# Softmax totals of a gated cross-attention block: a VectorE sum of block-transposed p and one 16-column fp32 matmul, in place of two 512-column matmuls with a matrix of ones

## What is computed

```python
q = rope((layernorm(x) @ Wq).reshape(b, t, 32, 128))
k = rope((ctx @ Wk).reshape(b, t, 8, 128));  v = (ctx @ Wv).reshape(b, t, 8, 128)
logits = 30 * tanh(einsum('btkgd,bTkd->bkgtT', q, k) * 0.0884 / 30)
weights = softmax(where(mask, logits, -1e30), axis=-1)
x = x + tanh(g_xattn) * (einsum('bkgtT,bTkd->btkgd', weights, v).reshape(b, t, 4096) @ Wo)
# then x = x + tanh(g_ffn) * ffn(layernorm(x)), a gated silu block, inner size 1376, int4 weights
```

## Time and profile before

| what | value |
|---|---|
| median of 3 runs (lowest, highest) | 819.16 us (818.01 to 819.62) |
| the profiled execution: time, span | 819.05 us, 817.3 us |
| mean granted TensorE clock | 0.991 |
| PE busy | 785.6 us (96%) |
| DVE busy | 586.6 us (72%) |
| POOL busy | 492.8 us (60%) |
| ACT busy | 355.4 us (43%) |

### The profile page before, as it was taken

How to read it: one execution, slowest core, us unless ns; L and a number is a source line. 1 busy time by engine, 2 the same in 40 slices (tenths; PEclk the granted TensorE clock), 3 DMA queues, 4 the chain that set the end, 5 groups by cost and what they waited for, 6 DMA issues and landing times.

```text
span 817.3 us, 12587 instructions
## 1 busy us (share of the span) xinstructions
PE 785.6 (96%) x3937; PEld 654.8 (80%) x3937; DVE 586.6 (72%) x1224; ACT 355.4 (43%) x722; POOL 492.8 (60%) x392
## 2 busy tenths in 40 slices
PE   4889999999999999999999999999998689999998
PEld 3777888888888888888888888888887468888786
DVE  7797777777777777777777777776787677787531
ACT  3665444444334444444443443434444345555420
POOL 3689765566555666655665566656887466566400
PEclk9999999999999999999999999999999899999999
DMA  8320302010210201020102101120020034442011
GB/s 286 108 78 17 115 1 78 1 52 1 78 54 1 78 1 52 1 78 0 55 1 78 52 0 43 35 47 1 1 62 0 25 88 103 101 111 49 1 65 39
DMA packets 56989, 41.61 MB, mean 51 GB/s; under 512 B 22922, under 2 KB 44298, under 8 KB 56938
## 3 DMA queue, kind: packets, MB, share of 16 engines
q1 hardware_dynamic: 56938, 40.90, 17.3%
HBM read 38.77 MB, written 2.11 MB: 50 GB/s over the span
## 4 chain that ended last, share of the span: by engine, by line
PE 91%; DVE 5%; POOL 2%; issue 1%; ACT 1%; DMA 0%; DVEq 0%; POOLq 0%
PE ps_o L53 8%; PE ps_o L55 8%; PE ps_o L54 7%; PE bank_q L55 7%; PE bank_q L53 7%; PE bank_q L54 7%; PE ps_qT L1141 3%; PE bank_kv L53 3%; PE bank_kv L54 3%; PE bank_kv L55 3%; PE ps_s L54 3%; PE ps_s L53 3%; PE ps_s L55 3%; PE ps_pv L53 2%; PE ps_pv L54 2%; PE ps_pv L55 2%
## 5 line engine op out<-in xcount | busy, mean ns | idle before, releaser
L522 POOL TENSOR_TENSOR aT_lo<-attn,aT_hi 128x512 fp32r<-128x512 f32 x64 | 96.6, 1510 | 168.4 <-ACT aT_hi L691 168.4
L651 ACT CAST qT_hi<-ps_qT 128x512 fp32r<-128x512 f32 x64 | 37.5, 585 | 169.7 <-PE bank_kv L1142 90.0
L53 PE MATMUL bank_q<-wq_hi,xT_hi 128*128 128x512 f32 x256 | 107.7, 421 | 1.0 <-DVE wq_lo L819 1.0
L53 PE MATMUL ps_o<-wo_hi,aT_hi 128*128 128x512 f32 x256 | 100.6, 393 | 2.5 <-POOL aT_lo L522 1.8
L55 PE MATMUL bank_q<-wq_hi,xT_lo 128*128 128x512 f32 x256 | 102.3, 400 | 0.0
L54 PE MATMUL bank_q<-wq_lo,xT_hi 128*128 128x512 f32 x256 | 102.3, 400 | 0.0
L55 PE MATMUL ps_o<-wo_hi,aT_lo 128*128 128x512 f32 x256 | 99.9, 390 | 0.0
L54 PE MATMUL ps_o<-wo_lo,aT_hi 128*128 128x512 f32 x256 | 99.8, 390 | 0.0
L507 POOL TENSOR_TENSOR probs<-probs,keepT 128x512 f32<-128x512 f32 x64 | 83.1, 1299 | 13.0 <-ACT probs L667 13.0
L535 POOL TENSOR_TENSOR roped<-q_cos,q_sin 128x512 f32<-128x512 f32 x61 | 78.8, 1293 | 1.8 <-DVE q_sin L840 1.7
L911 DVE TENSOR_TENSOR qT_lo<-ps_qT,qT_hi 128x512 fp32r<-128x512 f32 x64 | 44.2, 691 | 43.4 <-ACT kT_hi L652 43.4
(11 more groups left out here) (233 smaller groups left out, 2209.5 us busy)
## 6 DMA issues: line engine op xcount, KB each, us to landing
wo_raw<-in_Wo SPq DMA_DIRECT2D x8, 1024.0 KB, 5.4
wq_raw<-in_Wq SPq DMA_DIRECT2D x7, 1024.0 KB, 5.7
packed<-in_gate_q SPq DMA_DIRECT2D x40, 64.0 KB, 2.3
packed<-in_up_q SPq DMA_DIRECT2D x40, 64.0 KB, 2.3
packed<-in_down_q SPq DMA_DIRECT2D x10, 256.0 KB, 3.4
acc<-in_x SPq DMA_DIRECT2D x8, 256.0 KB, 8.1
wkv_raw<-in_Wk SPq DMA_DIRECT2D x8, 256.0 KB, 5.9
wkv_raw<-in_Wv SPq DMA_DIRECT2D x8, 256.0 KB, 6.3
```

Source lines behind the costliest of these rows:

```text
L53: nc.tensor.matmul(out, w_hi, m_hi, start=first, stop=False)
L522: nc.gpsimd.tensor_tensor(aT_lo[:], attn[:], aT_hi[:].bitcast(F32), ALU.subtract).then_inc(a_split, 1)
L651: nc.scalar.copy(qT_hi[:], ps_qT[:])
```

## The change

The 512-column sums over partitions leave PE. For slot s-2 DVE turns the masked p (fp32, not its halves) in 32x32 blocks straight from `probs`, and sums each block's 32 columns: `partial` (128x16) then holds, for each of the four groups of 32 partitions, the sum over the 32 keys of that group. One fp32 matmul of 16 columns with the stationary matrix `fold` adds the four groups and puts the total in the place where the block transposition of `ps_tot` had it, so that transposition goes, and the reciprocal reads PSUM. `fold` (a 1 where row and column agree modulo 32) is made on DVE from the identity, where POOL set `ones` before. ACT's exp has a further wait, for `p_turned`, because DVE now reads `probs` too.

```diff
+        fold = sb("fold", [P, P], F32)
+        partial = sb("partial", [P, GC // 32], F32)
...
-                nc.gpsimd.memset(ones[:].bitcast(F32), 1.0).then_inc(ones_done, 1)
...
                     wait(act, tanh_done, j + 1)
                     wait(act, p_split, j - 1)
+                    wait(act, p_turned, j - 1)
...
                 norm_moments(2)
+                dve.wait_ge(id_done, 1)
+                nc.vector.reduce_sum(r_tot[:, 0:32], ident[:].rearrange("p (i c) -> p c i", i=4), AX_X).then_inc(fold_done, 1)
+                dve.wait_ge(fold_done, 1)
+                nc.vector.tensor_copy(fold[:].rearrange("p (i c) -> p i c", i=4),
+                                      r_tot[:, 0:32].unsqueeze(1).to_broadcast([P, 4, 32])).then_inc(fold_done, 1)
                 dve.wait_ge(keep_T, 1)
...
+                    if runs(s - 2):
+                        wait(dve, masked, j - 1)
+                        wait(dve, norm_done, j - 2)
+                        nc.vector.transpose(r_tot[:], probs[:, (s - 2) % 2, :]).then_inc(p_turned, 1)
+                        wait(dve, p_turned, j - 1)
+                        wait(dve, tot_done, j - 2)
+                        nc.vector.reduce_sum(partial[:], r_tot[:].rearrange("p (c e) -> p c e", e=32), AX_X).then_inc(p_summed, 1)
                     if runs(s):
                         wait(dve, q_done, j + 1)
...
-                        nc.vector.transpose(r_tot[:], ps_tot[:]).then_inc(tot_turned, 1)
-                        wait(dve, tot_turned, j - 1)
-                        nc.vector.reciprocal(r_small[:], r_tot[:].rearrange("p (c e) -> p c e", e=32)[:, :, 0]).then_inc(inverted, 1)
+                        nc.vector.reciprocal(r_small[:], ps_tot[:, 0:GC // 32]).then_inc(inverted, 1)
...
-                pe.wait_ge(ones_done, 1)
+                pe.wait_ge(fold_done, 2)
...
-                        nc.tensor.matmul(ps_tot[:], ones[:], p_hi[:], start=True, stop=False)
-                        nc.tensor.matmul(ps_tot[:], ones[:], p_lo[:], start=False, stop=True).then_inc(tot_done, 1)
+                        wait(pe, p_summed, j - 1)
+                        nc.tensor.matmul(ps_tot[:, 0:GC // 32], fold[:], partial[:], start=True, stop=True).then_inc(tot_done, 1)
```

More of the change, by code:

```diff
@@ L160, in flamingo_block @@
         dead = sb("dead", [P, 1], F32)
-        ones = sb("ones", [P, P], F32R)
+        fold = sb("fold", [P, P], F32)
+        partial = sb("partial", [P, GC // 32], F32)
         r_tot = sb("r_tot", [P, GC], F32)
@@ L224, in flamingo_block @@
         ld_wq, ld_wkv, ld_wo = sem("ld_wq"), sem("ld_wkv"), sem("ld_wo")
-        id_zero, id_done, ones_done, half_done = sem("id_zero"), sem("id_done"), sem("ones_done"), sem("half_done")
+        id_zero, id_done, half_done = sem("id_zero"), sem("id_done"), sem("half_done")
         stats_done, moments_done, var_done = sem("stats_done"), sem("moments_done"), sem("var_done")
@@ L241, in flamingo_block @@
         tot_done, inverted, norm_done = sem("tot_done"), sem("inverted"), sem("norm_done")
-        tot_turned, r_spread = sem("tot_turned"), sem("r_spread")
+        p_turned, p_summed, r_spread, fold_done = sem("p_turned"), sem("p_summed"), sem("r_spread"), sem("fold_done")
         a_rounded, a_split, o_done, acc_done = sem("a_rounded"), sem("a_split"), sem("o_done"), sem("acc_done")
```

## The result

The changed kernel takes **821.58 us** (median of 7 runs, 820.48 to 821.9) where the kernel before takes 819.16 (7 runs, 818.01 to 820.51): 1.0026 times as long, 95% interval 1.0016 to 1.0036. So it is slower by 2.4 us. I had forecast 825.0, slower by 6. The profiled execution has a span of 819.9 us at a mean granted clock of 0.987 (before 817.3 us, 0.991).

The account below looks back on a forecast made before the run. PE was taken to bound the slots, with PE following DVE at the start. 819.05 + 7.1 (start, slots 2 and 3) - 57 x (0.46 - c), with c = 0.44, gave 825.0 us; range 811 to 838.

Parts of the forecast that it names:

- the start: Before the slots: the first q matmul waits for `fold` on DVE and delays all behind it, +6.2 us.
- my 0.85: Slots 2 and 3: DVE sets the pace, so its added work and a late `partial` cost +0.85 us.
- DVE in the steady slots: Net DVE work grows 0.6 to 0.7 us in a slot of 9.35 us and fits its idle time.
- four times: 0.44: `ps_tot` matmul on PE: four passes, each priced as an fp32 transposition with its load, 0.11 us; 0.44 a slot.
- c: PE's added time per slot for the fp32 matmul of 16 columns, in us; ends 0.12 and 0.75, taken as 0.44.
- the first rival: `ps_tot` matmul: passes with the same half of `fold` share a load, two loads, 0.22 us; 812.5 us, chance 0.27.
- The way I had named to read c: In the changed kernel's trace, the step from `ps_tot`'s start to `ps_pv`'s is PE's added matmul time.
- the steady slot taken for all of slots 4 to 61: 57 slots of 64 were each counted as saving PE 0.46 us less the added matmul's time.
- 1.2 us of cover: In a slot, the sum on DVE ends at 323.22 and PE reaches `ps_tot` at 324.48, so PE doesn't wait.
- no value: Last two slots, where the drain runs over ACT and POOL: PE's saving was not counted.
- nothing behind gives it back: After the late first q matmul, all later start-up work hangs on this chain, so the +6.2 us stay.
- slot 3 alone should show it: Sign in the trace: PE's wait for `partial` appears in slot 3 only, not in steady slots.

Follow-up runs that it names:

- e1: The changed kernel with `fold` made first on DVE, ahead of the first norm: 815.73 us.
- e2: The changed kernel with a loop body of 48 slots instead of 16, so no jump back between slots: 817.31 us.
- e12: The changed kernel with a loop body of 8 slots instead of 16, five jumps back; doesn't compute the layer: 817.60 us.
- e7: The kernel before with DVE's added transposition and sum of p alone, their result unused: 823.86 us.
- e5: The changed kernel with the 16-column fp32 matmul done twice in each slot: 835.62 us.
- e6: The changed kernel with `fold` and `partial` held in fp32r, so the totals are rounded: 813.38 us.
- e3: The kernel before with a loop body of 48 slots instead of 16: 819.42 us.
- e10: The changed kernel with `fold` made first and a loop body of 48 slots, the last three slots' totals made as in the kernel before: 807.90 us.
- e4: The changed kernel with `ps_pv` ahead of `ps_tot` on PE: 820.87 us.

## Why the prediction was right and wrong

**Right: the start.** The first q matmul ran at 17.47 us (forecast 17.4) behind `fold`, `q_cos` at 23.09 (22.8), `prep(2)` at 27.87 (27.2), slot 0's transpositions 6.14 us later (6.2). e1 gives all of it back (+0.05 for slot 1). The pace of the q matmuls was as assumed (0.43 us each). Slots 2 and 3 cost 0.2 us in this trace: slot 2 lost 0.63, with a wait of 1.32 us for `partial` in it, and slot 3 gained 0.41, without one. In e2 and e12, the same code up to there, they cost 1.0, so my 0.85 was about right and the 0.2 is one trace's; by slot 5 the three stand at +6.3 to +6.8. The wait for `partial`, which I had put into slot 3 with 0.25 us, came in slot 2 with 1.32 and in slot 4 with 0.21.

**Right: DVE in the steady slots.** The reduction took 0.69 us, the transposition 0.70, and no PE wait for `partial` stands from slot 5 to 23; e7's steady slots are unchanged. The idle time in the earlier trace rows had room for both.

**Wrong: the step "four times: 0.44".** c is 0.24 us. This term was mis-sized, by 57 x 0.2 = 11.4 us, and the first rival's *two loads* describe it (c = 0.22): 128 load records for 64 matmuls, each worth about 0.12 us; e5 adds the same 0.24 again, and e6 with one load costs 0.10. The rival's reason, that two passes share a load, fits two records; that four passes lie behind them no row shows. The Trainium skill ("FP8 and Floating Point Precision", TensorE Precision Notes) speaks of four passes for fp32: in time the trace shows twice an fp32r product, not four times. The unit that I multiplied, 0.11 us for a load with its matmul, was about right; the number of loads wasn't. The fp32 transpositions could not have told me, since each is one record in the kernel before. The way I had named to read c, from `ps_tot`'s start to `ps_pv`'s, shows only 0.13 us: the rest lies in `ps_pv`, whose load isn't covered. Only the slot's length shows it whole.

**Wrong: the steady slot taken for all of slots 4 to 61.** By the first rival's sum the time would be 812.5. It is 9 us more because two places are not steady slots:
- the jumps back, +4.9 us (1.88 + 3.47, less the 0.46 that before had there). I had 1.2 us of cover for `partial` (it was 1.1) and never asked what a jump takes from it: DVE's gap took 1.7, the slow `p_lo` 1.05, and the clock 1.6 more at the second. Shown by e2 (4.3 us back), e3 and e12; in e1's trace the jumps cost 2.8, so the size isn't a constant.
- the last slots, +3.6 us. I had "no value" for PE's saving there, but not a loss, though DVE carries the second norm there, and the work I added to it was costed only beside a steady slot's idle time. Shown by e7, which loses 3.0 us there, and e10, which gets 2.8 back.

*Sum of what was measured:* 819.05 + 6.3 (start to slot 5) - 57 x 0.22 + 4.9 + 3.6 = 821.3; measured 821.6. So the direction was right and the size wrong, and the size was that near only by luck: the two errors, -11.4 and +8.5 us, have opposite signs (with a start 0.8 cheaper than forecast they lead from 825.0 to 821.3). The statement "nothing behind gives it back" held. The sign "slot 3 alone should show it" failed: seven places show the wait, and slot 3 isn't one of them.

**Open:** what exactly makes DVE's jump take 2.3 us with 272 instructions and not with 256 or fewer; why PE idles 0.8 us at e1's jumps and not at those of the changed kernel; why e4's steady slot is 0.04 us longer; and whether the clock falls behind such a wait in general: it fell in the changed kernel behind the second one of 1.63 us and not behind the first one of 1.65, nor behind e6's two of 1.65.

## What to carry to other kernels

A gain that holds in 57 equal slots was eaten by three places that aren't equal: the start, the loop's seams, the drain. Before costing work that moves to a second engine, look at its idle time in each of these, not only in the steady slot, and treat a new wait as something that turns that engine's hiccups into those of the bounding one. A constant that the bounding engine will wait for goes first in its maker's order. And when a trace lacks an operation, measure it alone before it is multiplied by 57.

## What the runs showed of the hardware

- An fp32 matmul of 16 columns with a 128x128 stationary is two weight loads and two matmuls and costs 0.22 to 0.24 us of PE's path; in fp32r it is one of each and 0.10.
- DVE's jump back with a body of 272 or 288 instructions left it without one for 2.2 to 2.6 us (all twelve jumps of the changed kernel, e1, e4, e5, e6 and e7), with 256 for at most 0.93, and with 136 for 0.65, about as in any slot.
- PE's gap at a jump changed with its code unchanged: none in the changed kernel, 0.76 and 0.85 us in e1.
- The granted clock fell to the lower level for about 3.4 us behind one idle time of 1.63 us of PE, after some 146 us without any, and didn't behind three of 1.65; the fall took another 1.6 us.
- `p_lo` on DVE took 1.73 us instead of 0.68 when it began 0.11 us behind POOL's `wq_lo`; when it began 0.05 us ahead of it (e5), `wq_lo` took 1.79 us instead of 1.29. So a late engine can be late by more than its gap.
